# The quantised SwiGLU moved into the last head pair of the grouped attention, on one core

## The reference, cut to what matters

```python
x = x + tanh(g_xattn[1]) * _L1_xattn_ref(_layernorm(x), ctx, ctx, mask, wq, wk, wv, wo, 0)
x = x + tanh(g_ffn[1]) * _L1_ffn_ref(_layernorm(x), w_gate, s_wgate, w_up, s_wup, w_down, s_wdown, inv_gate, inv_up, inv_inter)

def _dynamic_quant(x, inv_smooth):
    xs = x.astype(float32) * inv_smooth
    scale = maximum(max(abs(xs), axis=-1) / QMAX, 1e-08)
    q = clip(round(xs / scale), -QMAX, QMAX)
    return (q, scale)
# _L1_ffn_ref, rows of 512 in bfloat16, inner width 256
qg, sg = _dynamic_quant(x_flat, inv_gate)
qu, su = _dynamic_quant(x_flat, inv_up)
gate_out = (qg @ w_gate.T) * sg * s_wgate
up_out = (qu @ w_up.T) * su * s_wup
inter = clip(silu(gate_out) * up_out, -10, 10).astype(bfloat16)
qi, si = _dynamic_quant(inter, inv_inter)
out = (qi @ w_down.T) * si * s_wdown
```

## Time and profile before

| | |
|---|---|
| median of 3 runs | 873.41 us (869.49 to 873.47) |
| the profiled execution | 871.6 us, its span 869.8 us |
| busy, share of the span | PE 781.7 us (90%), DVE 678.1 (78%), POOL 364.6 (42%), ACT 354.0 (41%) |
| TensorE's weight loads (PEld) | 615.0 us (71%), beside its matmuls |
| mean granted TensorE clock | 0.965 of full speed |

### The profile page before, as it was taken

How to read it: one execution, slowest core, us unless ns; L and a number is a source line. 1 busy time by engine, 2 the same in 40 slices (tenths; PEclk the granted TensorE clock), 3 DMA queues, 4 the chain that set the end, 5 groups by cost and what they waited for, 6 DMA issues and landing times. The chain is left out here.

```text
span 869.8 us, 12638 instructions
## 1 busy us (share of the span) xinstructions
PE 781.7 (90%) x4276; PEld 615.0 (71%) x4276; DVE 678.1 (78%) x1250; ACT 354.0 (41%) x1063; POOL 364.6 (42%) x300
## 2 busy tenths in 40 slices
PE   2899988878799999999999999999999999994674
PEld 1555554766688878888778888878888887763562
DVE  5888887778787787777878777787777777876994
ACT  2777775221233424334243333433433333243552
POOL 2777777215543433224344233343332332203662
PEclk9999999998899999999999999999999999997897
DMA  8310030101021111101121010111111102002001
GB/s 255 98 48 24 24 102 1 37 0 49 19 56 49 42 43 38 36 25 37 37 61 37 25 37 25 49 37 41 46 30 32 37 13 55 1 1 72 13 36 48
DMA packets 37444, 37.41 MB, mean 43 GB/s; under 512 B 2897, under 2 KB 27217, under 8 KB 37393
## 3 DMA queue, kind: packets, MB, share of 16 engines
q1 hardware_dynamic: 35168, 32.81, 12.7%
q10 hardware_dynamic: 2224, 3.94, 1.5%
HBM read 34.64 MB, written 2.10 MB: 42 GB/s over the span
## 5 line engine op out<-in xcount | busy, mean ns | idle before, releaser
L923 POOL TENSOR_TENSOR dense<-rope_a,rope_b 128x512 f32<-128x512 f32 x62 | 79.4, 1281 | 189.1 <-DVE rope_b L1036 189.1
L976 ACT ACTIVATE ot_hi<-PB 128x512 fp32r<-128x512 f32 x64 | 38.4, 600 | 211.3 <-PE PB L1281 211.3
L1195 PE MATMUL QB<-xT_hi,wq_lo 128*128 128x512 f32 x256 | 107.8, 421 | 2.4 <-DVE xT_lo L1109 2.4
L967 ACT ACTIVATE e_sb<-masked,nmax 128x64 f32<-128x64 f32 x256 | 86.5, 340 | 56.0 <-DVE nmax L1065 55.3
L1195 PE MATMUL ROW<-wo_hi,ot_lo 128*128 128x512 f32 x256 | 102.0, 398 | 2.9 <-DVE ot_lo L1083 2.6
L1033 DVE TENSOR_TENSOR rope_a<-QB,rope 128x512 f32<-128x512 f32 x62 | 42.9, 692 | 78.3 <-PE QB L1197 78.1
L1196 PE MATMUL QB<-xT_lo,wq_hi 128*128 128x512 f32 x256 | 102.3, 400 | 0.0
L1197 PE MATMUL QB<-xT_hi,wq_hi 128*128 128x512 f32 x256 | 102.0, 399 | 0.0
L1196 PE MATMUL ROW<-wo_lo,ot_hi 128*128 128x512 f32 x256 | 101.6, 397 | 0.0
L1197 PE MATMUL ROW<-wo_hi,ot_hi 128*128 128x512 f32 x256 | 101.1, 395 | 0.0
L1036 DVE TENSOR_TENSOR rope_b<-QB,rope 64x512 f32<-64x512 f32 x124 | 85.4, 689 | 3.9
(11 more groups left out here) (202 smaller groups left out, 1905.4 us busy)
## 6 DMA issues: line engine op xcount, KB each, us to landing
raw<-in_wq SPq DMA_DIRECT2D x32, 256.0 KB, 2.8
raw<-in_wo SPq DMA_DIRECT2D x32, 256.0 KB, 2.6
ctx_two<-in_ctx SPq DMA_DIRECT2D x16, 256.0 KB, 3.7
x_sb<-in_x SPq DMA_DIRECT2D x8, 256.0 KB, 8.1
ctx_raw<-in_ctxT ACTq DMA_DIRECT2D x1, 2048.0 KB, 12.9
raw<-in_wv SPq DMA_DIRECT2D x8, 256.0 KB, 2.7
raw<-in_wk SPq DMA_DIRECT2D x8, 256.0 KB, 3.0
out<-x_sb SPq DMA_DIRECT2D x8, 256.0 KB, 2.0
```

The source lines that it names most:

```text
L923: nc.gpsimd.tensor_tensor(dst, a, b, ALU.add).then_inc(s_rot, 1)
L967: nc.scalar.activation(e_sb[:, r, :], masked[:, r, :], ACT.Exp, bias=nmax[:, r:r + 1], accum_out=zsum[:, r:r + 1]).then_inc(s_exp, 1)
L1195: nc.tensor.matmul(out, lhs[1], rhs[0], start=first, stop=False)
```

## The change

`grouped_attention` becomes `attention_and_swiglu`, and `quantised_swiglu` as a block goes. The last pair has its own stream on each engine, `last`, of 22 steps: the 16 slots and 6 more. Tile t has its row statistics in step 10+t, is smoothed, quantised, clipped and transposed in 11+t, goes through gate and up, tanh and `inner` in 12+t, the inner quantisation in 13+t, and `down` and the addition in 14+t. Silu is written with tanh, which shares its factors with the scales. The row factors and the last gate are multiplied into the weights ahead of it (`fold_*`), in steps 7 to 10, and the weights are split in steps 10 (gate, up) and 11 (down) by ScalarE and GpSimd. The two clips move from VectorE to GpSimd. VectorE adds the down product to x_sb itself. The SwiGLU has no tiles of its own: its weights lie in those of the keys and values and in the context, its sums in banks of the attention. Apart from that, each score matmul takes only the 64 keys of its batch, in all pairs.

```diff
+        xs = [w.rearrange("p k i -> p (k i)").rearrange("p (n i) -> p n i", n=2) for w in wgu_raw]
...
+        TQ, GU, TI = QB, KV, TB
+        LAST = PAIRS - 1
+        STATS, SMOOTH, GATE, INTER, DOWN = range(10, 15)
+        STEPS = DOWN + TILES
...
+        def down_bank(t):
+            return PB2[:, 0, :] if t + DOWN < SLOTS else SB_[:, :]
...
+            sp.wait_ge(s_v, 8 * PAIRS)
+            for n, name in enumerate(("w_gateT", "w_upT")):
+                sp.dma_start(wgu_raw[n], d[name].rearrange("(k p) n -> p k n", p=P)).then_inc(s_wgu, 16)
             sp.wait_ge(s_piece, PIECES * PAIRS)
             load_rows(sp, d, c)
+            sp.wait_ge(s_k, 4 * PAIRS)
+            for k in range(IC):
+                sp.dma_start(wd_raw[k], d["w_downT"][P * k:P * k + P, :]).then_inc(s_wd, 16)
...
+                pool.wait_ge(c["s_rows"], 96)
+                nc.gpsimd.tensor_scalar(row_gu[0], row_gu[0], 0.5, None, ALU.mult).then_inc(s_fold, 1)
+                nc.gpsimd.tensor_tensor(row_d, row_d, tg[:, 3:4].broadcast_to([P, D]), ALU.mult).then_inc(s_fold, 1)
...
+            def fold_gate_up(n):
+                pool.wait_ge(s_wgu, 32)
+                pool.wait_ge(s_fold, 2)
+                nc.gpsimd.tensor_tensor(wgu_raw[n], wgu_raw[n], row_gu[n].unsqueeze(1).broadcast_to([P, KC, INNER]),
+                                        ALU.mult).then_inc(s_fold, 1)
+            def fold_down(k):
+                pool.wait_ge(s_wd, 32)
+                nc.gpsimd.tensor_tensor(wd_raw[k], wd_raw[k], row_d, ALU.mult).then_inc(s_fold, 1)
...
+            def clip(t):
+                pool.wait_ge(s_qm, 2 * t + 2)
+                nc.gpsimd.tensor_scalar(xs[t % 2], xs[t % 2], ROUND + QMAX, ROUND - QMAX, ALU.min, ALU.max)\
+                  .then_inc(s_clip, 1)
...
+            def last():
+                for n in range(STEPS):
+                    if (t := ffn_tile(n, SMOOTH)) is not None:
+                        smooth(t)
...
+                    if n == 7:
+                        fold_rows()
+                    if n in (8, 9):
+                        fold_gate_up(n - 8)
+                    if n == 10:
+                        for i in range(2):
+                            weight_rest(i, wgu[1][i], wgu_raw[i], wgu[0][i])
+                    if (t := ffn_tile(n, INTER)) is not None:
+                        inner_clip(t)
+                    if (t := ffn_tile(n, SMOOTH)) is not None:
+                        clip(t)
+                    if (t := ffn_tile(n, GATE)) is not None:
+                        inner_smooth(t)
+                    if (t := ffn_tile(n, STATS)) is not None:
+                        inverse_deviation(nc, pool, c, s_var, s_rstd, t, t + 1, 3 + t)
+                    if n == 10:
+                        for k in range(IC):
+                            fold_down(k)
+                    if n == 11:
+                        for k in range(IC):
+                            weight_rest(2 + k, wd[1][k], wd_raw[k], wd[0][k])
...
+            def gate(t):
+                act.wait_ge(s_gu, t + 1)
+                if t:
+                    act.wait_ge(s_prod, t)
+                else:
+                    act.wait_ge(s_rot, q_job(LAST, 11) + 1)
+                nc.scalar.activation(th, GU[:, 0:INNER], ACT.Tanh, scale=sc[:, t % 2, 0:1]).then_inc(s_th, 1)
...
+            def last():
+                for n in range(STEPS):
...
+                    if n <= SLOTS:
+                        round_pt(N - 1)
+                    if n < SLOTS:
+                        exps(N)
+                    if (t := ffn_tile(n, INTER)) is not None:
+                        inner_quantise(t)
+                    if (t := ffn_tile(n, SMOOTH)) is not None:
+                        quantise(t)
+                    if (t := ffn_tile(n, GATE)) is not None:
+                        gate(t)
+                    if n <= SLOTS:
+                        round_ot(N - 1)
+                    if (t := ffn_tile(n, INTER)) is not None:
+                        inner_to_stationary(t)
+                    if (t := ffn_tile(n, SMOOTH)) is not None:
+                        to_stationary(t)
...
+                    if n == 10:
+                        act.wait_ge(s_k, 4 * PAIRS)
+                        for i in range(2):
+                            act.wait_ge(s_fold, 3 + i)
+                            nc.scalar.activation(wgu[0][i], wgu_raw[i], ACT.Copy).then_inc(s_fhi, 1)
+                    if n == 11:
+                        for k in range(IC):
+                            act.wait_ge(s_fold, 5 + k)
+                            nc.scalar.activation(wd[0][k], wd_raw[k], ACT.Copy).then_inc(s_fhi, 1)
...
-                own = SB_[:, :].rearrange("p (a r k) -> p r a k", a=4, r=2)[:, :, 0:4:3, :]
+                own = SB_[:, 0:4 * S].rearrange("p (b r k) -> p r b k", b=2, r=2)
...
+            def to_bf16(t):
+                dve.wait_ge(s_rstd, 3 + t)
+                nc.vector.tensor_scalar(xb[:, :], x_sb[:, t, :], mv[:, t, 0:1], rstd[:, t, :],
+                                        ALU.subtract, ALU.mult).then_inc(s_xb, 1)
...
+            def inner(t):
+                dve.wait_ge(s_th, t + 1)
+                nc.vector.scalar_tensor_tensor(out=th, in0=th, scalar=1.0, in1=GU[:, 0:INNER],
+                                               op0=ALU.add, op1=ALU.mult).then_inc(s_m, 1)
+                dve.wait_ge(s_m, t + 1)
+                dve.wait_ge(s_scgu, t + 1)
+                nc.vector.scalar_tensor_tensor(out=prod, in0=GU[:, INNER:2 * INNER], scalar=sc_gu[:, t % 2:t % 2 + 1],
+                                               in1=th, op0=ALU.mult, op1=ALU.mult).then_inc(s_prod, 1)
+                dve.wait_ge(s_prod, t + 1)
+                if t:
+                    dve.wait_ge(s_xi, t)
+                nc.vector.tensor_scalar(ib[:, :], prod, SWIGLU_LIMIT, -SWIGLU_LIMIT, ALU.min, ALU.max)\
+                  .then_inc(s_ib, 1)
...
+            def add_down(t):
+                dve.wait_ge(s_dn, t + 1)
+                nc.vector.scalar_tensor_tensor(out=x_sb[:, t, :], in0=down_bank(t), scalar=sci[:, t % 2:t % 2 + 1],
+                                               in1=x_sb[:, t, :], op0=ALU.mult, op1=ALU.add).then_inc(s_x, 1)
...
+            def last():
+                nc.vector.memset(magic[:, :], ROUND).then_inc(s_magic, 1)
+                for n in range(STEPS):
+                    N = SLOTS * LAST + n
+                    if n < SLOTS:
+                        mask_and_max(N, n % 8)
+                    if n <= SLOTS:
+                        rest_pt(N - 1)
+                    if n < 12:
+                        rope_q(q_job(LAST, n), N + 4, n % 4)
+                    if (t := ffn_tile(n, INTER)) is not None:
+                        inner_scales(t)
+                    if (t := ffn_tile(n, SMOOTH)) is not None:
+                        scales(t)
+                    if n < SLOTS:
+                        normalize(N)
+                    if (t := ffn_tile(n, GATE)) is not None:
+                        inner(t)
+                    if (t := ffn_tile(n, DOWN)) is not None:
+                        add_down(t)
+                    if n <= SLOTS + 1:
+                        accumulate(N - 2, (n - 2) % 8)
+                    if (t := ffn_tile(n, STATS)) is not None:
+                        stats(t)
+                    if n <= SLOTS:
+                        rest_ot(N - 1)
+                    if (t := ffn_tile(n, STATS)) is not None:
+                        to_bf16(t)
...
-                out = SB_[:, :].rearrange("p (kb r k) -> p kb r k", kb=2, r=4)
                 for b in range(2):
                     for r in range(2):
                         q = q_rot[:, unit % 2, 2 * i + b, 2 * r:2 * r + 2, :].rearrange("p h s -> p (h s)")
-                        mm = nc.tensor.matmul(out[:, :, 2 * b + r, :], q,
-                                              keys.rearrange("p (kb k) -> p kb k", kb=2), start=True, stop=True)
+                        a = 2 * b + r
+                        mm = nc.tensor.matmul(SB_[:, S * a:S * a + S], q, keys[:, S * b:S * b + S],
+                                              start=True, stop=True)
...
+                    if n < SLOTS:
+                        score(LAST, N, n)
...
+                    if n < SLOTS:
+                        if (t := ffn_tile(n, DOWN)) is not None:
+                            down(t)
+                        if (t := ffn_tile(n, GATE)) is not None:
+                            gate_up(t)
+                    if n <= SLOTS + 1:
+                        outputs(N - 2)
+                    if n <= SLOTS:
+                        if n in (DOWN, DOWN + 1):
+                            pe.wait_ge(s_x, n - DOWN + 1)
+                        weighted(N - 1)
...
+                    if (t := ffn_tile(n, INTER)) is not None:
+                        inner_transposes(t)
+                    if (t := ffn_tile(n, SMOOTH)) is not None:
+                        q_transposes(t)
```

500 lines of the change are left out of this document (204 added, 296 removed).

## The result

The changed kernel takes 865.2 us (median of 4 runs, 864.98 to 865.92) against 873.44 for the kernel before (869.49 to 873.52): ratio 0.992, 95% interval 0.990 to 0.994. The forecast was 865. Run again beside the last three experiments it gave 0.994 (0.991 to 0.996).

| | before | forecast | after |
|---|---|---|---|
| first score matmul of the attention | 235.09 | unchanged | 236.66 |
| from there to slot 10 of the last pair | 509.46 | -3.2 | 506.39 (-3.07) |
| C1, slot 10's start to Q11, the end of the first `quantise` | | 23.4 | 22.4 |
| C2, Q11 to Q12 | | 13.0 | 12.9 |
| C3, Q12 to Q18 (forecast with step 17's 0.5, which lies in it) | | 66.9 | 67.0 |

The account below looks back on a forecast made before the run. TensorE's own stream was taken to bound the kernel up to slot 10 of the last pair, chains over four engines after it. 871.6 - 3.2 (score) - 3.75 (last stretch) = 864.6, forecast 865 us, range 855 to 874.

Parts of the forecast that it names:

- C1: From slot 10's start to the end of the first `quantise`, in step 11: 23.4 us.
- C2: From the end of `quantise` in step 11 to that in step 12, including the first clip: 13.0 us.
- C3: `quantise` end in step 12 to that in step 18: two steps of 10.6 us, four of 11.3, together 66.4.
- step 17's 0.5: Added to the last pair's steps because down, gate and up stand behind the last outputs on TensorE: 0.5 us.
- C4: From the end of `quantise` in step 18 to the kernel's end: 18.2 us.
- Part A: Score matmuls read 64 keys instead of 128; weight loads set the pace, 0.055 us a slot, 3.2 us gained.
- R1: Rival: the score matmuls follow their columns, gaining about 24 us, time 844 us; chance 0.10.
- Part B: GpSimd's folds of row factors into weights, steps 7 to 9, ahead of slot 10: covered by TensorE's stream, 0.
- The ring: Closed chain in the last steps from one `quantise` to the next: 10.6 us, 11.3 with `add_down` from step 14.
- What would show it: Trace signs: score to transposes 0.84 us, `quantise` every 11.3 us from step 14, TensorE gaps, wide clip 1.7 us.
- R2: Rival: GpSimd, sharing with VectorE, sets the last steps' pace; `smooth` products at 1.85 us, time 877 us; chance 0.11.
- R3: Rival: work overlaps but nothing is gained; steps 0.6 us longer, score gives 0, time 871 us; chance 0.14.

Follow-up runs that it names:

- the last three experiments: Three kernels combining edits to the changed kernel (down weights' folds and rests moved, VectorE/GpSimd reordered, later gate and up rests earlier): 852.2, 848.4 and 848.7 us.
- b3: Changed kernel with ScalarE's gate and up roundings at the head of step 10 and both GpSimd rests ahead of that step's rotation: 863.9 us, ratio 0.991.
- b2: Changed kernel with the down weights' folds moved into step 11 and their rests into step 12, between `smooth` and `clip`: 862.6 us, ratio 0.990.
- g2: Changed kernel with b2's edit, `add_down`, `accumulate`, `stats` ahead of `inner`, both gate/up folds in step 8, roundings and one rest earlier: 848.4 us, ratio 0.973.
- b1: Changed kernel with GpSimd's inverse deviation of tile 0 ahead of the gate and up weights' rests in step 10: 866.2 us, ratio 0.992.

## Why the prediction was right, point by point

The mechanism was the one named: the loads' pace in the score, and one closed chain over four engines in the last steps. That the parts of the second half came out within 1 us each is in part luck, as told at C2, C3 and C4.

- **Part A.** Right to 0.1 us: 3.07 for 3.2, and 0.05 us a slot. R1 is dead: with half the columns, seven of the eight distances between records are still the 0.11 us that their loads have, and one fell to 0.06. The Trainium skill, "TensorE: Matmul & The Clock Gate", section "Back-to-back issue gap", says that in a stream of loads and matmuls both set the spacing, and gives columns over the clock plus 2.5 ns for a matmul by itself only. The trace agrees that the loads count; its 0.11 us a record for f32 is longer than the page's 81 ns for 128 columns.
- **Part B.** No price. Slots 8 and 9 are as long as before, less 0.05. But one fold ran in slot 10, and b3 showed that it stands in the way of the rounding and the rests there. "Covered" was true of TensorE's stream and not of GpSimd's own queue.
- **C1.** 22.4 for 23.4. The rests took 4.77 for 5.2, and a hop between engines 0.05. The moved folds (b2) and the rests moved earlier (g2) confirm that the terms are on the path: 1.2 and 3.7 us less. Of the folds' 2.6 us in the sum moving them won less than half.
- **C2.** 12.9 for 13.0, by two errors that cancel. The clip took 1.04, at the lower bound and not 1.7 (the 0.9 estimated from what the Trainium skill, "GPSIMD Engine Reference", section "4.1 Engine selection", says of one-input work was nearer). The eight transposes took 1.97 instead of 1.05, at the lower of the two clock levels (0.50 granted). The clock had fallen at 759.9 us, when TensorE had stood since 757.3; TensorE then worked for 1.0 us and stood for 5.58 more:

```profile
766.67 1.97 PE L1636 MATMUL QB<-ident,wgu_raw 128*128 128x128 f32 x8 [5.58 <-POOL wgu_raw L1046]
```

- **C3.** 67.0 for 66.9, again by errors that cancel. The ring is the one that was named, 10.25 for 10.6 and 10.9 with `add_down` for 11.3: over six steps 2.2 us less than forecast. Three steps were longer than it, by 2.7 together. One took 11.6: `weighted` waited 2.55 us for `add_down`, the score stood behind it and behind transposes at the low clock, and VectorE had to mask that score ahead of its scales. The clock made the difference and not the wait: the same step took 10.9 us in b1 and b2, where the clock was 1.00 and 0.99 and `weighted` waited 2.56 in b1, and 12.5 in the changed kernel's second profile, at 0.73. The last two steps are not the ring either: 11.6 and 12.4, where tanh waited 0.5 and 1.3 us for gate and up, which stand behind the outputs on TensorE. The 0.5 us added for this were too few; two steps lost 2.1 us to it.

```profile
826.84 0.51 PE L1475 MATMUL ROW<-wo_hi,ot_lo 128*128 128x512 f32 x1 [3.14 <-DVE ot_lo L1291]
```

- **C4.** 18.7 for 18.2. The clip was 0.66 shorter than forecast, and at a clock of 0.58 the eight transposes took 1.97 for 1.05 and gate and up 3.0 for 2.1.
- **What would show it.** Steps every 11 to 12 us from step 14, gaps of TensorE of 1.7 to 3.1 us, the clip behind ScalarE: yes. That `xb` waits for `rstd`: 4.03 us in step 10, 0.25 in step 11 and 0.67 in the last. In the ring `rest_ot` fills that time, and b1 shows that the one long wait was free. "At a clip of 0.9 the result is 863" was not borne out: the clip took 1.04, for which the same sum gives 863.3, and the profiled execution took 865.9, of which 1.57 come from its start. The transposes at the low clock took back most of what the clip gave.
- **R2** didn't decide: the `smooth` products took a median of 1.17 us each, as before, and none more than 1.19. The sharing that it named is there in the other direction: where GpSimd was given more to do, VectorE was held.
- **R3** had the ring 0.6 longer; it was 0.35 shorter.

## What to carry to other kernels

When stages of one kernel are laid into another's slots, sum the ring through all queues before the work: a step can't be shorter than the longest closed chain, and what closes it may be only an order. Here VectorE's additions and statistics stood behind `inner`; another order of the same operations won 9.8 us with no work removed. And follow what an idle engine waits for before taking that wait away: the longest one was free.

## What the runs showed that was not expected

- VectorE is held while GpSimd works, until the end of GpSimd's instruction, and for some operations only. `ib` 0.29 became 1.03 beside a clip, `xb` 0.55 became 1.48 beside a fold, a scale of 2 columns 0.17 became 1.07 beside a rest, each ending when the operation on GpSimd had ended. The reduction `am`, 1.22, and `accumulate`, 0.74, which reads PSUM, kept their times. The Trainium skill, "SBUF — State Buffer", section "SBUF: two separate sides", names an exclusive lock between a GpSimd instruction and one of VectorE that is in a two-port mode or reads two SBUF inputs, held for the whole instruction. These rows agree as far as they show it; in which mode an operation of VectorE ran no row says.
- A one-input clip of 1024 columns on GpSimd takes as long, 1.04 us, as a product of 512 columns with a broadcast operand.
- The start of the attention moved by 5.4 us between executions whose code is the same up to there. Differences of less than about 3 us were seen in the traces, from a common point on, and not in the times.
